# Moving the normalised rows of attention and routing from VectorE to ScalarE in a fused MoE, attention, MoE kernel

## The reference, cut to what matters

```python
x = x + 0.5 * ffn(layernorm(x))     # layer 0 of routing
x = x + attn(layernorm(x))
x = x + 0.5 * ffn(layernorm(x))     # layer 1 of routing

# ffn: LayerNorm again (with gamma, beta), router logits of 8 experts,
#   the two best experts of each row with softmax gates, each expert
#   silu(gate) * up -> down with 384 hidden, and one shared expert with 128 hidden
# attn: windows of 128 rows; q, k, v; scores = q k^T / sqrt(128); the 32 largest
#   scores of each row are kept, softmax over them; out = attn v;
#   out = leaky_relu(out); r = out + x; LayerNorm(r) * gamma + beta
```

## Time and profile before

| | us |
|---|---|
| median of 3 runs (lowest, highest) | 652.7 (650.8, 653.05) |
| profiled execution, its own time | 650.28 |
| its span, first to last instruction | 648.5 |
| mean granted TensorE clock | 0.912 |

### The profile page before, as it was taken

One profiled execution on the slowest core, in us unless ns is written; L12 is line 12 of the kernel. 1 busy time (PEld: TensorE's weight loads), 2 busy tenths in 40 slices (PEclk: granted clock), 3 DMA queues, 4 the chain that ended last, 5 costly groups with the idle time before them and its releaser, 6 DMA issues.

```text
span 648.5 us, 15350 instructions
## 1 busy us (share of the span) xinstructions
PE 510.9 (79%) x3928; PEld 464.5 (72%) x3928; DVE 426.7 (66%) x1893; ACT 296.5 (46%) x694; POOL 353.7 (55%) x515
## 2 busy tenths in 40 slices
PE   2775998967898988999983099883579997879990
PEld 2463898867798988979782087872478996879980
DVE  6556785751787626789899848999577864164223
ACT  1222444434458644574743057452365446435540
POOL 1450587777543754337677412767047878543550
PEclk9965999987899999999997589998599999999995
DMA  7994457446754578535503264412435567698734
GB/s 203 294 169 139 165 169 271 161 143 180 257 196 154 198 243 290 189 132 171 186 30 98 70 217 146 151 64 67 154 125 190 201 212 238 231 330 292 259 135 154
DMA packets 87971, 117.88 MB, mean 182 GB/s; under 512 B 11800, under 2 KB 60832, under 8 KB 87888
## 3 DMA queue, kind: packets, MB, share of 16 engines
q1 hardware_dynamic: 75120, 96.35, 45.8%
q0 software_dynamic: 9312, 19.16, 9.5%
q10 hardware_dynamic: 3456, 1.38, 0.9%
HBM read 26.57 MB, written 26.19 MB: 81 GB/s over the span
## 4 chain that ended last, share of the span: by engine, by line
PE 48%; DMA 13%; issue 11%; POOL 10%; DVE 7%; SPq 6%; ACT 4%; ACTq 1%; POOLq 0%; DVEq 0%
PE ps_g L624 10%; PE ps_y L639 10%; PE ps_u L629 5%; PE ps_h L629 5%; POOL rows L1426 5%; DMA xin<-rows 4%; POOL results L1454 4%; DMA yg<-results 3%; DMA raw_dn<-in_dnw 3%; SPq L383 2%; PE ps_x L618 2%; PE w L569 2%; PE ps_s L543 2%; DVE pr L1239 2%; DVE xres L1187 2%
## 5 line engine op out<-in xcount | busy, mean ns | idle before, releaser
L1454 POOL DMA_INDIRECT results<-raw_gu,idx x163 | 160.3, 984 | 147.7 <-ACT raw_gu L813 88.5
L639 PE MATMUL ps_y<-dn_t,raw_gu 128*128 x978 | 140.3, 281 | 15.8 <-ACT raw_gu L813 15.7
L624 PE MATMUL ps_g<-x_t,raw_dn 128*128 128x128 f32 x978 | 141.0, 282 | 7.4 <-issue 7.4
L1426 POOL DMA_INDIRECT rows<-zz,s_idx x128 | 124.6, 974 | 38.9 <-issue 26.5
L639 PEld LDWEIGHTS ps_y<-dn_t,raw_gu 128*128 128x128 f32 x978 | 124.5, 194 | 23.6 <-issue 23.1
L624 PEld LDWEIGHTS ps_g<-x_t,raw_dn 128*128 128x128 f32 x978 | 125.1, 196 | 12.5 <-issue 12.1
L813 ACT COPY raw_gu<-ps_y 128x128 f32<-128x128 f32 x163 | 43.0, 264 | 140.2 <-PE ps_y L639 130.4
L804 ACT ACTIVATE x_t<-ps_x,bf_c,gf_c 128x128 f32<-128x128 f32 x163 | 75.2, 461 | 46.7 <-PE ps_x L618 46.2
L808 ACT ACTIVATE sil<-ps_g 128x384 f32<-128x384 f32 x163 | 79.9, 490 | 28.3 <-PE ps_g L624 27.3
L1255 DVE TENSOR_TENSOR raw_gu<-sil,ps_h 128x384 f32<-128x384 f32 x81 | 44.7, 552 | 66.4 <-PE ps_h L629 47.8
L1255 DVE TENSOR_TENSOR raw_gu<-sil,ps_u 128x384 f32<-128x384 f32 x82 | 45.3, 552 | 57.9 <-PE ps_u L629 52.2
...
## 6 DMA issues: line engine op xcount, KB each, us to landing
raw_dn<-gu_t SPq DMA_DIRECT2D x163, 384.0 KB
xin<-rows SPq DMA_DIRECT2D x163, 64.5 KB
...
results<-raw_gu,idx POOLq DMA_INDIRECT x163
...
rows<-zz,s_idx POOLq DMA_INDIRECT x128
...
```

The lines of the kernel that those rows point to most:

```text
L624: t = pe.matmul(ps_g[:, c, :], ws[:, k4, c * P:(c + 1) * P], x_t[:, k, :], start=True, stop=True)
L639: t = pe.matmul(ps_y[:, 0, :], h_t[:, k4, c * P:(c + 1) * P], dn[:, bass.ds(off + c * D, D)], start=(c == 0), stop=(c == FC - 1))
L1426: pool.indirect_dma_start(xs, bass.IndirectOffsetOnAxis(s_idx[n][:, c, k:k + 1], 0), zz[n][:, k, c, :], None).then_inc(scat[n], 16)
L1454: pool.indirect_dma_start(yt, bass.IndirectOffsetOnAxis(idx[:, k8:k8 + 1], 0), yb[:, k4, :], None).then_inc(yst[k4], 16)
```

## The change

1. The normalised rows `zz` (both layers) and `xn` are made by ScalarE: `activation(Identity, scale = rstd, bias = nmr)`, one for each tile. VectorE makes the bias with one small operation for each Newton chain (`centre`), which signals `nd`. ScalarE's program has `norm_z` and then `norm_x` behind `mix` and ahead of `turn_z`; no block part stands between the eight activations. In layer 0 the rows of R + 1 stand ahead of the shared expert's Silu of R, except where a new chain of statistics is due.
2. `mix` copies the attention output tile by tile with scale `rinv`: four copies of 128 columns instead of one of 512. It waits for `ri_done` too.
3. The residual is one `tensor_tensor` of 512 columns instead of four `scalar_tensor_tensor` of 128.
4. Because ScalarE now reads `mv`, `rstd` and `nmr`, VectorE's second Newton operation (n = 1) waits until the rows of the chain before are made (`xn_done`, `z_done`).
5. All five weaves are set anew. Blocks whose gate matmuls PE has been given, counted from the two PE weaves:

| ahead of | before | after |
|---|---|---|
| scores of step 2 | 65 | 65 |
| scores of step 3 | 73 | 70 |
| scores of step 4 | 83 | 78 |
| step 5 | 85 | 85 |
| scores of step 6 | 95 | 92 |
| scores of step 7 | 102 | 100 |
| `turn_z` of step 8 | 110 | 108 |
| end of step 9 | 123 | 120 |

On GpSimd the 8 scatters of J = 4 have no block result between them before, and four after (those of blocks 98 to 101, behind the second, third and fourth piece). The 8 scatters of J = 2 have none before and none after.

The diff, without the numbers of the weaves:

```diff
--- before.py
+++ after.py
@@ -89,26 +89,27 @@
 WEAVE = {
...
-VALUES, ROUTE_ROWS, NEXT_ROWS, AFTER, AFTER_LATE, PICKS, SHARED, SHARED_LATE = 9, 11, 12, 13, 12, 19, 26, 31
+VALUES, AFTER, AFTER_LATE, PICKS, SHARED, SHARED_LATE = 9, 13, 12, 19, 26, 31
@@ -214,7 +215,7 @@
         var_e = sb("var_e", [P, NT])
...
         nw_t = sb("nw_t", [P, NT])
-        nmr = sb("nmr", [P, TB])
+        nmr = sb("nmr", [P, NT])
         zz = [sb(f"zz{n}", [P, TB, 2, XW]) for n in range(RING)]
         nz_t = sb("nz_t", [P, TB, P])
@@ -289,7 +290,7 @@
         cst, pc, pad_z = sem("cst"), sem("pc"), sem("pad_z")
         wt_ps, wt_a, wt_v = sem("wt_ps"), sem("wt_a"), sem("wt_v")
-        bn1, ag1, bn2, ag2, bn3, ag3, nw, nw2 = (sem(n) for n in ("bn1", "ag1", "bn2", "ag2", "bn3", "ag3", "nw", "nw2"))
+        bn1, ag1, bn2, ag2, bn3, ag3, nw, nw2, nd = (sem(n) for n in ("bn1", "ag1", "bn2", "ag2", "bn3", "ag3", "nw", "nw2", "nd"))
         z_done, ids = sem("z_done"), sem("ids")
         nzT_ps, nzT_sb, lg_ps, lg_sb = (sem(n) for n in ("nzT_ps", "nzT_sb", "lg_ps", "lg_sb"))
@@ -341,15 +342,34 @@
             eng.sem_inc(passed[eng.engine], 1)
+        def stages(s):
+            return tuple(s - n if 0 <= s - n < STEPS else None for n in range(3))
+        def following(s):
+            return s + 1 if s + 1 < STEPS and s + 1 not in LATE else None
+        chain_alone, chain_at, rows_before = {}, {}, {}
+        c, n_x, n_z = FIRST_NORMS, 0, STEPS
+        def alone(p):
+            nonlocal c, n_x
+            rows_before[c], chain_alone[p] = (n_x, n_z), c
+            c, n_x = c + 1, n_x + 1
+        alone(0)
+        for s in range(STEPS + 2):
+            p, J = following(s), stages(s)[2]
+            if p is not None or J is not None:
+                rows_before[c], chain_at[s] = (n_x, n_z), c
+                c, n_x, n_z = c + 1, n_x + (p is not None), n_z + (J is not None)
+            if s + 1 in LATE:
+                alone(s + 1)
         ps_us = (ps_u, ps_h)
-        def stages(s):
-            return tuple(s - n if 0 <= s - n < STEPS else None for n in range(3))
-        def following(s):
-            return s + 1 if s + 1 < STEPS and s + 1 not in LATE else None
         def stored_by(B, k):
@@ -727,14 +747,42 @@
                 act.copy(gu_t[:, e, 0:FF], ff((ps_g, ps_x)[e % 2])).then_inc(wt_a, 1)
                 act.copy(dn_t[:, e, :], ff(ps_h)).then_inc(wt_a, 1)
+            def norm_x(p, chain):
+                act.wait_ge(nd, chain + 1)
+                if p >= XRING:
+                    act.wait_ge(rr_done, p - XRING + 1)
+                for k in range(TB):
+                    act.activation(xn[p % XRING][:, k, :], xres[:, p * TB + k, :], ACT.Identity,
+                                   bias=nmr[:, k:k + 1], scale=rstd[:, k:k + 1]).then_inc(xn_done, 1)
+                    turn()
+            def norm_z(R, tile, col, chain):
+                act.wait_ge(nd, chain + 1)
+                if R >= RING:
+                    act.wait_ge(scat[R % RING], R // RING * N_SCAT)
+                for k in range(TB):
+                    src = xres[:, tile + k:tile + k + 1, :].broadcast_to([P, 2, D])
+                    act.activation(zz[R % RING][:, k, :, 0:D], src, ACT.Identity,
+                                   bias=nmr[:, col + k:col + k + 1], scale=rstd[:, col + k:col + k + 1]).then_inc(z_done, 1)
+                    turn()
+            def first_rows(R):
+                norm_z(R, R * TB, R * TB, max(n for n in range(FIRST_NORMS) if FIRST_CHAINS[n] <= R))
             def turn_p(A):
...
                 act.wait_ge(o_ps, A + 2)
+                act.wait_ge(ri_done, A + 1)
                 act.wait_ge(lr_done, A + 1)
-                act.copy(o[:], w1[:]).then_inc(o_sb, 1)
+                for k in range(TB):
+                    t = act.activation(o[:, k, :], w1[:, k, :], ACT.Copy, scale=rinv[:, k:k + 1])
+                t.then_inc(o_sb, 1)
             def turn_x(a):
                 act.wait_ge(xnT_ps, a + 1)
@@ -769,7 +817,7 @@
                 act.wait_ge(x2_done, A + 1)
...
                     act.activation(rn[:, k, :], rr[:, k, :], ACT.Identity,
-                                   bias=nmr[:, k:k + 1], scale=rstd[:, AFTER_AT + k:AFTER_AT + k + 1]).then_inc(rn_done, 1)
+                                   bias=nmr[:, AFTER_AT + k:AFTER_AT + k + 1], scale=rstd[:, AFTER_AT + k:AFTER_AT + k + 1]).then_inc(rn_done, 1)
                     turn()
             def shared(R):
@@ -818,14 +866,21 @@
                 act.wait_ge(cb, C * N_CB + 3 * N_CB)
                 act.dma_start(out[tile:tile + TB].rearrange("t p d -> p t d"), xres[:, tile:tile + TB, :]).then_inc(out_st, 16)
+            turn()
+            first_rows(0)
             turn_z(0)
...
             for R in range(STEPS):
+                late = R and R + 1 in FIRST_CHAINS
+                if R + 1 < STEPS and not late:
+                    first_rows(R + 1)
                 shared(R)
...
                 if R + 1 < STEPS:
+                    if late:
+                        first_rows(R + 1)
                     turn_z(R + 1)
...
                     logits(R + 1, (R + 1) * TB)
@@ -834,7 +889,8 @@
             gates_of_layer(0)
...
                 (a, A, J), p = stages(s), following(s)
-                if s == 0 or s in LATE:
+                if s in chain_alone:
+                    norm_x(s, chain_alone[s])
                     turn_x(s)
...
                     queries(s)
@@ -847,8 +903,13 @@
                 if A is not None:
...
                     turn()
+                if A is not None:
                     mix(A)
                     turn()
+                if J is not None:
+                    norm_z(STEPS + J, J * TB, ROUTE_AT, chain_at[s])
+                if p is not None:
+                    norm_x(p, chain_at[s])
                 if J is not None:
...
                     turn()
@@ -919,7 +980,7 @@
                 stats(lambda k: res(tile, k), 0, bn1, ag1, a * TB, turn)
             def stats_after(A):
-                dve.wait_ge(rr_done, A * TB + TB)
+                dve.wait_ge(rr_done, A + 1)
                 apart(dve)
                 stats(lambda k: rr[:, k, :], AFTER_AT, bn2, ag2, A * TB, turn)
@@ -958,6 +1019,10 @@
                 if n == N_NORM - 1:
                     dve.wait_ge(chain, at + N_NW)
+            def centre(lo, hi, done):
+                dve.scalar_tensor_tensor(nmr[:, lo:hi], mv[:, lo:hi, 0], -1.0, rstd[:, lo:hi], ALU.mult, ALU.mult).then_inc(done, 1)
             def norms_after(n, A):
                 if n == 0:
@@ -965,8 +1030,7 @@
                 if n < N_NORM:
...
                 else:
-                    dve.scalar_tensor_tensor(nmr[:], mv[:, AFTER_AT:AFTER_AT + TB, 0], -1.0, rstd[:, AFTER_AT:AFTER_AT + TB],
-                                             ALU.mult, ALU.mult).then_inc(nw2, 1)
+                    centre(AFTER_AT, AFTER_AT + TB, nw2)
             def first_stats(R):
@@ -980,23 +1044,8 @@
                 for m in range(N_NORM):
...
                     turn()
-            def norm_x(n, tile):
-                for k in range(TB):
-                    dve.tensor_scalar(xn[n][:, k, :], res(tile, k), mv[:, k, 0:1], rstd[:, k:k + 1],
-                                      ALU.subtract, ALU.mult).then_inc(xn_done, 1)
-                    turn()
-            def norm_z(R, n, tile, col, used=True):
-                if used:
-                    dve.wait_ge(scat[n], R // RING * N_SCAT)
-                for k in range(TB):
-                    src = xres[:, bass.ds(tile + k, 1), :].broadcast_to([P, 2, D])
-                    dve.tensor_scalar(zz[n][:, k, :, 0:D], src, mv[:, col + k, 0:1], rstd[:, col + k:col + k + 1],
-                                      ALU.subtract, ALU.mult).then_inc(z_done, 1)
-                    turn()
+                centre(lo, hi, nd)
+                turn()
             def bc(t):
                 return t.rearrange("p (t o) -> p t o", o=1).broadcast_to([P, TB, NE])
@@ -1195,10 +1244,8 @@
                 dve.scalar_tensor_tensor(lr[:], o[:], SLOPE, o[:], ALU.mult, ALU.max).then_inc(lr_done, 1)
...
                 dve.wait_ge(rn_done, A * TB + TB)
-                for k in range(TB):
-                    dve.scalar_tensor_tensor(rr[:, k, :], lr[:, k, :], rinv[:, k:k + 1], xn[n][:, k, :],
-                                             ALU.mult, ALU.add).then_inc(rr_done, 1)
-                    turn()
+                dve.tensor_tensor(rr[:], lr[:], xn[n][:], ALU.add).then_inc(rr_done, 1)
+                turn()
             def values(a):
                 dve.wait_ge(v_ps, a + 1)
@@ -1274,11 +1321,7 @@
                     first_stats(J)
                 first_norms(n, lo * TB, hi * TB)
-            def first_rows(R):
-                norm_z(R, R, R * TB, R * TB, used=False)
             first_chain(0)
-            first_rows(0)
             dve.wait_ge(wt_ps, 1)
             dve.tensor_copy(sm_t[:, 3:6, :], w1[:, 0:3, :])
@@ -1289,16 +1332,12 @@
```

(48 more changed lines are left out.)

12 lines of the change are left out of this document (3 added, 9 removed).

## The result

The changed kernel takes 645.3 us in the median of 20 runs (643.5 to 652.0), the kernel before 651.1 of 20 (648.1 to 653.1) on the same chip: ratio 0.9925, 95% interval 0.9904 to 0.9946. That is faster by more than the 0.5% that can be told, and 2.3 us above the predicted 643.0. The profiled execution has a span of 645.0 us against 648.5.

A forecast was written before the change was run, and what follows sets the result against it. VectorE was taken to bound steps 2 to 6, ahead of two walls. Gains of 7.3 + 5.6 + 4 + 3 less costs of 4, 5.1 and 1 gave 9.8 us: 652.7 to 642.9, predicted 643, range 633 to 656.

The forecast's parts named there:

- What bounds it: VectorE bounds steps 2 to 6; PE and GpSimd bound layer 0 and 460 to 632 us; two walls between.
- The relief of VectorE: Steps 2 to 6: VectorE loses 2.8 us in each full step (2, 3, 5, 6), 1.7 in step 4.
- The first wall: 356.5 to 373 us, PE nearly idle after step 4: 7.3 us gained ahead of it by VectorE's shorter steps 2 to 4.
- moved blocks: Blocks moved into step 4 and the second wall fill idle time: 4 us gained in steps 2 to 4, 3 in 5 and 6.
- The second wall: 440.3 to 460 us, PE nearly idle: 5.6 us plus 3 gained ahead, 5.1 lost to four block results between J = 4's scatters.
- Layer 0's third step: PE waits there for zz, and ScalarE's four rows, centre and one hop make it later: cost 1 us.
- Rival 3: ScalarE's bursts of rows, 35 us together, stall PE's blocks; slower if over 39% shows, 660 us at 60%; chance 0.14.
- Rival 2: Full steps: ScalarE becomes late, its burst entered two blocks late, costing 10 us and not 4: 648.9 us; chance 0.17.
- Rival 4: PE paces the search and GpSimd's scatters the walls, so VectorE's freed time becomes idle: 652 us; chance 0.12.

The follow-up runs named there:

- e6: The changed kernel with both zz and xn of the attention loop made by VectorE again: 650.2 us, ratio 0.9930 to the kernel before.
- e5: The changed kernel with only zz of the attention loop made by VectorE again, xn on ScalarE: 638.7 us, ratio 0.9768 to the kernel before.
- e4: The changed kernel with four block results moved behind the eight scatters of J = 4 on GpSimd: 649.0 us, ratio 0.9901 to the kernel before.
- e8: The changed kernel itself, run again beside its variants: 649.4 us, ratio 0.9921 to the kernel before.
- e3: The changed kernel with only xn of the attention loop made by VectorE again, zz on ScalarE: 646.4 us, ratio 0.9866 to the kernel before.

## Why the prediction was right, and what was not

*What bounds it.* VectorE in steps 2 to 6: right for 5 and 6 in number (61.3 to 55.4 us, predicted 55), and only a third for 2 to 4 (92.5 to 89.2, predicted 83). Layer 0 kept its length, and the walls were where the text had them. Its sentence that both walls end with VectorE's work and a tail of scatters held, but for 0.9 us in the first, by which GpSimd's queue is later than the places.

*The relief of VectorE.* Its busy time fell by 35.8 us (predicted 30), and the 6 us too many are luck: `pr` fell from 18.6 to 12.5 us because it met GpSimd's additions less often (it is 15.1 us in e6 and 10.7 in e5, by timing alone). That is 2.1, 1.4 and 2.2 us in steps 2, 3 and 5, beside the 2.8 us a step that the change itself takes off, and it stands in no term. The prediction had met the two engines' exclusion at a GpSimd issue, for 0.11 us, and left it out of the sum; at `pr` it is ten times as large. How much of it shortened the steps no run separates; PE waited for VectorE's `xres` at the next scores by 0.2, 0.4, 1.8 and 0.9 us before (steps 3, 4, 6, 7). The prices of single operations were right: `rr` 0.69 (0.68), `zz` 0.59 on ScalarE (0.58), four in 2.08 (2.05), ScalarE's 60 us by sums of means too (37.9 + 15.4 + 7.1). No table load was added. `mix` took 1.14 and not 1.5.

*The first wall, 7.3 us + 4 for moved blocks - its share of the waits:* measured nothing (block 85 at 373.5 against 373.3). This is the term that failed, in two places. The burst: ScalarE's cost was priced as VectorE waiting 1 us for logits, and there is no such wait in steps 2, 3, 5 and 6. It shows at PE, which waits for `zz` and `xn`, 1.3 to 1.8 us a full step. And step 4, which was to lose 1.7 us and to take the moved blocks into PE's idle time: it starts 5 blocks and not 1, and from its scores to block 85 it is 49.2 us and not 44.3. These 4.9 us are 3.1 to VectorE's places (30.5 against 27.4), 0.9 in GpSimd's queue, which is busy 25.5 of 30.6 us with the results of the blocks among its work (19.8 of 27.5 before), and 0.8 behind the first dispatch. In the 3.1 VectorE is busy 0.6 us more, with the products of the blocks, and waits 3.9 us in the step and not 1.4: 2.1 at such products and 0.9 for GpSimd's `xres`. That these waits come from the moved blocks is read from the rows and not tested, and the last 0.8 stays open.

*The second wall, 5.6 + 3 - 5.1:* block 102 one us later than before. The wall is 6.9 us longer (predicted 5): 5.5 between the first and the last dispatch, near the 5.1 of the term, and 1.4 ahead of them. But the four results can't be taken back for as much: e4 takes 5.5 us off and 1.7 arrive, since PE's routing work is right behind. What paid is behind the wall, where the prediction had nothing: 4.3 us less from block 102 to the last, with 3.7 us less of PE's work there, which now stands in the wall.

*Layer 0's third step:* no cost; the transposes of `zz` start at 55.2 and not at 56.0, and step 0's scores come at 178.5 as before.

*The rivals.* Rival 3, the bursts stall the blocks, was at work in the full steps: PE's waits for rows are 6.1 us more there, of 14.8 us of bursts (41%). In layer 0 they did not grow, and in the second wall they are hidden, so it is 17% of all 35 us and not the 39% at which it would have decided. Removing its dearer half (e5) gained another 10 us on that chip, part of it by the burst. The Trainium skill, *ScalarE: Activation LUTs*, "Rules for kernel authors", prefers VectorE for plain add and multiply. The runs agree for the wide rows (e5 against e8). For the narrow ones it depends on what else VectorE has: e3 is no slower than the changed kernel, but e6, where VectorE has all, is 1.6% behind e5. Rival 2 did not come: no VectorE wait for the logits, and PE's waits for ScalarE's block parts did not grow in sum (`x_t` 3.5 to 6.7 us, the copy of results 15.7 to 12.3). Rival 4 had the half of it that counts, that the walls turn freed time into idle time.

*The sum.* 9.8 us forecast, 5.8 by medians, 3.5 in the profiled span. The total is right within its range by luck in part: it is made up of a first wall that came 9.5 us worse than forecast, waits that were counted at the wrong engine, and a gain behind the second wall for which there was no term.
